# Attention's gathered tables hold two vector components twice, and the sum of a tile's rows is one operation

## The reference

```python
s_n, v_n = _equiv_layernorm(s, v, gamma_s, beta_s, gamma_v)
msg_s = (s_n @ Ws_src)[src] + (s_n @ Ws_dst)[dst]
msg_v = einsum('ncx,cd->ndx', v_n, Wv_src)[src] + einsum('ncx,cd->ndx', v_n, Wv_dst)[dst]
m1_s, m1_v = _cg_tp(msg_s, msg_v, y0, y1, ...)   # products with y, a dot and a cross product of msg_v and y1
a = ...                                          # one logit an edge and head, from m1_s
alpha = softmax of a over the edges with the same dst
h = ...                                          # values an edge, from m1 through a second _cg_tp
agg = segment_sum(alpha * h, dst)
```

## Time and profile before

| what | before |
|---|---|
| median of 3 runs | 25516.59 us |
| lowest and highest | 25451.02 and 25548.4 us |
| span of the profiled execution | 25427.1 us |
| its own time beside the span | the page gives none but the span |
| busy in the span: PE, DVE, ACT, POOL | 19679.3, 19154.8, 12590.5, 12879.8 us |
| node stage ahead of attention | about 6212 to 6580 us of the span |
| edge stage of attention | about 6580 to 17446 us of the span |

### The profile page before, as it was taken

The page is one execution under the profiler, slowest core; times in us unless marked ns, Lnnn a source line. Parts: engine busy times, 40 slices in busy tenths (PEclk is TensorE's granted clock), DMA queues, the critical chain, the costliest instruction groups (busy, mean ns, idle before and its releaser), DMA issues. The chain is left out here.

```text
span 25427.1 us, 480526 instructions
## 1 busy us (share of the span) xinstructions
PE 19679.3 (77%) x108650; PEld 15218.6 (60%) x108650; DVE 19154.8 (75%) x58214; ACT 12590.5 (50%) x42770; POOL 12879.8 (51%) x13907
## 2 busy tenths in 40 slices
PE   1466566565888889899989899985677799677799
PEld 1223222223677777778778777774555588555588
DVE  8333588887777778788878787878777688777688
ACT  0233344443577777777777777773333322333322
POOL 2777655664444444444444444442777500777500
PEclk6677788888999999999999999997999999999999
DMA  0466555555322222222222222223222200222200
GB/s 34 138 172 172 139 111 110 109 109 113 113 73 73 72 74 74 73 74 76 76 73 76 72 76 74 74 74 88 66 61 61 48 6 7 66 61 61 48 6 6
DMA packets 1776894, 1962.61 MB, mean 77 GB/s; under 512 B 754160, under 2 KB 1451744, under 8 KB 1776192
## 3 DMA queue, kind: packets, MB, share of 16 engines
q0 software_dynamic: 567456, 1314.26, 19.5%
q1 hardware_dynamic: 1209376, 647.65, 11.0%
HBM read 1399.54 MB, written 561.06 MB: 77 GB/s over the span
## 5 line engine op out<-in xcount | busy, mean ns | idle before, releaser
L1521 PE MATMUL e_sums<-e_feat,e_same 128*128 128x272 f32 x13824 | 3438.4, 403 | 1357.7 <-ACT e_feat L1542 1231.4
L1503 POOL DMA_INDIRECT e_rows<-x,e_take x3456 | 3609.3, 1044 | 1120.4 <-issue 1047.2
L1521 PEld LDWEIGHTS e_sums<-e_feat,e_same 128*128 128x128 f32 x13824 | 2593.6, 192 | 2202.1 <-issue 1590.7
L581 PE MATMUL e_sums<-e_feat,e_same 128*128 128x480 f32 x3456 | 1962.0, 724 | 1357.2 <-DVE e_feat L649 1357.2
L1049 PE MATMUL e_ps_m<-ident,e_m 128*128 128x128 f32 x12960 | 2092.9, 286 | 1073.6 <-ACT e_m L1122 1062.0
L565 POOL DMA_INDIRECT e_rows<-table,e_take x1728 | 1933.0, 1119 | 1347.0 <-issue 1300.8
L1116 ACT ACTIVATE e_m<-e_th,e_yt 128x64 f32<-128x64 f32 x6480 | 2324.4, 430 | 186.6 <-issue 9.4
L1049 PEld LDWEIGHTS e_ps_m<-ident,e_m 128*128 128x128 f32 x12960 | 1452.8, 145 | 1449.5 <-DVE e_m L1245 772.5
L581 PEld LDWEIGHTS e_sums<-e_feat,e_same 128*128 128x128 f32 x3456 | 803.0, 244 | 2516.8 <-issue 2411.3
L1007 POOL DMA_INDIRECT e_srow<-src_table,e_at x1620 | 1647.3, 1017 | 1248.9 <-POOL e_at L1002 952.5
L600 ACT ACTIVATE e_feat<-e_feat,e_pay 128x64 f32<-128x64 f32 x5184 | 1284.8, 334 | 1806.9 <-DVE e_feat L624 1717.1
(11 more groups left out here) (307 smaller groups left out, 53270.3 us busy)
## 6 DMA issues: line engine op xcount, KB each, us to landing
e_pay<-pay_rows SPq DMA_DIRECT2D x432, 470.0 KB, 3.9
order_keys<-key_row SPq DMA_DIRECT2D x810, 128.0 KB
e_keys<-key_row SPq DMA_DIRECT2D x1620, 64.0 KB, 3.0
e_rows<-x,e_take POOLq DMA_INDIRECT x3456, 2.6
order_feat<-in_attr_T SPq DMA_DIRECT2D x810, 64.0 KB, 3.6
comb<-n_comb SPq DMA_DIRECT2D x300, 164.0 KB, 1.9
e_rows<-table,e_take POOLq DMA_INDIRECT x1728, 4.0
pay_rows<-order_stage,order_put POOLq DMA_INDIRECT x1620
```

The costliest lines, as they stand in the source:

```text
L581: ins = pe.matmul(sums[b][q // G][:, 0:AGG0], same[b][:, q, :], feat[b][:, q, 0:AGG0], start=q % G == 0, stop=q % G == G - 1)
L1503: pool.indirect_dma_start(out=rows[t.j][:, q, :], out_offset=None, in_=x, in_offset=bass.IndirectOffsetOnAxis(ap=take[t.j][:, q:q + 1], ax ...
L1521: ins = pe.matmul(sums[b][q // G][:, 512 * h:512 * h + HALF], same[b][:, q, :], feat[b][:, q, h * HALF:(h + 1) * HALF], start=q % G == 0, ...
```

## The change

The projection part of the tables gets 64 more columns. `MSG` = D + 2 x CV = 224 columns hold the scalars and x y z x y; `COMB` becomes 224 + 168 = 392. The weight matrix `w1_tab` gets the blocks that yield x and y once more (`again`), so that `WT` is 2 x 448 wide instead of 2 x 320. `src_table`, `combs`, `ts`, `comb`, `srow` and `crow` get wider with it, and the four maxima and the sums in a comb row move 64 columns to the right. The two operations that sum a tile's rows become one of 224 columns.

```diff
-COMB = D + SMW
+MSG = D + 2 * CV
+COMB = MSG + SMW
...
-        WA, WX, WT = ph.sb("WA", [P, 4, 192]), ph.sb("WX", [P, 2, 192]), ph.sb("WT", [P, 2, 2 * D])
+        WA, WX, WT = ph.sb("WA", [P, 4, 192]), ph.sb("WX", [P, 2, 192]), ph.sb("WT", [P, 2, 2 * MSG])
...
-                            ins = pe.matmul(ps_c[:, 0:2 * D], nrmT[c.j][:, q * P:(q + 1) * P], WT[:, q, :], start=q == 0, stop=q == 1)
+                            ins = pe.matmul(ps_c[:, 0:2 * MSG], nrmT[c.j][:, q * P:(q + 1) * P], WT[:, q, :], start=q == 0, stop=q == 1)
...
-                        act.activation(ts[c.j][:, :], ps_c[:, 0:D], ACT.Copy)
-                        act.activation(comb[c.j][:, 0:D], ps_c[:, D:2 * D], ACT.Copy).then_inc(out_set, 1)
+                        act.activation(ts[c.j][:, :], ps_c[:, 0:MSG], ACT.Copy)
+                        act.activation(comb[c.j][:, 0:MSG], ps_c[:, MSG:2 * MSG], ACT.Copy).then_inc(out_set, 1)
...
-        srow = [ph.sb(f"srow{k}", [P, D]) for k in range(SLOTS)]
+        srow = [ph.sb(f"srow{k}", [P, MSG]) for k in range(SLOTS)]
...
-                        dve.tensor_tensor(mv[ka][:, 0:D], srow[a.j][:, :], crow[a.j][:, 0:D], ALU.add)
-                        dve.tensor_tensor(mv[ka][:, D:D + 2 * CV], srow[a.j][:, CS:CS + 2 * CV], crow[a.j][:, CS:CS + 2 * CV], ALU.add).then_inc(mv_set, 1)
+                        dve.tensor_tensor(mv[ka][:, :], srow[a.j][:, :], crow[a.j][:, 0:MSG], ALU.add).then_inc(mv_set, 1)
...
-                            sp.dma_start(runs[b.j][:, k, :], combs[k][where, D:COMB]).then_inc(runs_in[b.j], 16)
+                            sp.dma_start(runs[b.j][:, k, :], combs[k][where, MSG:COMB]).then_inc(runs_in[b.j], 16)
...
-        table0, src_table = dram("table0", [NP, D]), dram("src_table", [NP, D])
+        table0, src_table = dram("table0", [NP, D]), dram("src_table", [NP, MSG])
...
-    a["w1_tab"] = _blocks(256, 2 * D, [(0, 0, g["Ws_src"]), (0, D, g["Ws_dst"])]
-                          + _per_component(64, 64, g["Wv_src"]) + _per_component(64, D + 64, g["Wv_dst"]))
+    again = [(64 + CV * k, at + D + CV * k, w) for at, w in ((0, g["Wv_src"]), (MSG, g["Wv_dst"])) for k in range(2)]
+    a["w1_tab"] = _blocks(256, 2 * MSG, [(0, 0, g["Ws_src"]), (0, MSG, g["Ws_dst"])]
+                          + _per_component(64, 64, g["Wv_src"]) + _per_component(64, MSG + 64, g["Wv_dst"]) + again)
```

More of the change, by code:

```diff
@@ L732, in nodes_after_0 @@
         stats = [ph.sb(f"stats{k}", [P, 24]) for k in two]
-        ts = [ph.sb(f"ts{k}", [P, D]) for k in two]
+        ts = [ph.sb(f"ts{k}", [P, MSG]) for k in two]
         comb = [ph.sb(f"comb{k}", [P, COMB]) for k in two]
@@ L877, in _ @@
                     dve.memset(agg[k][:, AGG0:4 * P], 0.0)
-                    dve.memset(comb[k][:, D:D + 4], LOW)
-                    ins = dve.memset(comb[k][:, D + 4:COMB], 0.0)
+                    dve.memset(comb[k][:, MSG:MSG + 4], LOW)
+                    ins = dve.memset(comb[k][:, MSG + 4:COMB], 0.0)
                 ins.then_inc(blank, 1)
@@ L940, in edge_layer1 @@
         yt = [ph.sb(f"yt{k}", [P, 10]) for k in range(SLOTS)]
-        srow = [ph.sb(f"srow{k}", [P, D]) for k in range(SLOTS)]
+        srow = [ph.sb(f"srow{k}", [P, MSG]) for k in range(SLOTS)]
         crow = [ph.sb(f"crow{k}", [P, COMB + 4]) for k in range(SLOTS)]
-        mv, qs, qv = pair("mv", [P, CS + 5 * CV]), pair("qs", [P, 2 * CS]), pair("qv", [P, 3 * CV])
+        mv, qs, qv = pair("mv", [P, MSG]), pair("qs", [P, 2 * CS]), pair("qv", [P, 3 * CV])
         by_y1, by_y2, pairs = pair("by_y1", [P, 9 * CV]), pair("by_y2", [P, 9 * CV]), pair("pairs", [P, 4 * CV])
@@ L1159, in step @@
                         act.activation(hw[k][:, :].rearrange("p (h m) -> p h m", h=4)[:, :, 0:1], dif[k][:, 4:8].unsqueeze(2), ACT.Exp).then_inc(den_set, 1)
-                        act.activation(crow[c.j][:, D:D + 4], mx[k][:, 4:8], ACT.Copy).then_inc(kept, 1)
+                        act.activation(crow[c.j][:, MSG:MSG + 4], mx[k][:, 4:8], ACT.Copy).then_inc(kept, 1)
                     if a.exists():
@@ L1269, in step @@
                             dve.wait_ge(kept, c.count(-1))
-                        dve.tensor_tensor(mx[kc][:, 4:8], row[:, D:D + 4], mx[kc][:, 0:4], ALU.max).then_inc(mn_set, 1)
+                        dve.tensor_tensor(mx[kc][:, 4:8], row[:, MSG:MSG + 4], mx[kc][:, 0:4], ALU.max).then_inc(mn_set, 1)
                     if c.exists():
@@ L1274, in step @@
                             dve.wait_ge(ex_set, c.count(-1))
-                        old = row[:, D:D + 4]
+                        old = row[:, MSG:MSG + 4]
                         dve.tensor_tensor(dif[kc][:, :].rearrange("p (g h) -> p g h", g=2),
-                                          bass.AP(old.tensor, old.offset, [old.ap[0], [COMB - D, 2], [1, 4]]),
+                                          bass.AP(old.tensor, old.offset, [old.ap[0], [COMB - MSG, 2], [1, 4]]),
                                           bcast(mx[kc][:, 4:8].unsqueeze(1), (P, 2, 4)), ALU.subtract).then_inc(dif_set, 1)
@@ L1280, in step @@
                         dve.wait_ge(ex_set, c.count(1))
-                        acc = row[:, D + 4:COMB].rearrange("p (h m) -> p h m", h=4)
+                        acc = row[:, MSG + 4:COMB].rearrange("p (h m) -> p h m", h=4)
                         dve.tensor_tensor(acc, acc, bcast(ex[kc][:, 0:4].unsqueeze(2), (P, 4, HD)), ALU.mult).then_inc(scaled, 1)
@@ L1297, in step @@
                         dve.wait_ge(scaled, c.count(1))
-                        dve.tensor_tensor(row[:, D + 4:COMB], row[:, D + 4:COMB], ps_g[:, 0:4 * HD], ALU.add).then_inc(row_set, 1)
+                        dve.tensor_tensor(row[:, MSG + 4:COMB], row[:, MSG + 4:COMB], ps_g[:, 0:4 * HD], ALU.add).then_inc(row_set, 1)
                 run_steps(dve, step, 4, SLOTS, NT, COUNTS)
```

## The result

| | median | lowest to highest | runs |
|---|---|---|---|
| before | 25483.81 us | 25420.36 to 25548.4 | 4 |
| the change | 26455.18 us | 26430.02 to 26490.26 | 4 |

The ratio is 1.0389, with a 95% interval of 1.0367 to 1.0410. The change makes the kernel 971 us slower; 172 us slower was forecast.

The account below looks back on a forecast made before the run. The prediction took POOL's ring through the scatter's landing as the bound. It added 162 us at the edges and 10 us at the nodes, 172 us on 25516.6, for 25689 us, range 25530 to 25860.

Parts of the forecast that it names:

- What bounds the kernel: In the edge stage, POOL's ring of waits, closed by the scatter's landing, sets the pace: 6.72 us a tile.
- What is taken away: DVE's two sums at the edges become one of 391 ns: 0.07 to 0.15 us a tile, worth 0 on the path.
- What is added at the edges: Wider rows make the scatter land 0.10 us later a tile (bounds 0.06 and 0.19): 162 us in all.
- Rival 2: At the edges, the table gather delays the scatter, both growths adding: 0.19 us or more a tile, 25850 us; chance 0.10.
- Rival 3: In the edge stage, DVE sets the pace and tiles get 0.07 to 0.15 us shorter: 25404 to 25269 us; chance 0.08.
- Phase between DVE and POOL: Where POOL's operations fall against DVE's in the edge stage: gives or takes 40 us at most, left out of the sum.
- The nodes: In `nodes_after_0`, the wider table matmul and evictions add 10 us, bounds 0 and 30.

Follow-up runs that it names:

- e8: The kernel before with POOL's index copy split, so the source gather no longer waits for the scatter's landing; 24727.16 us, ratio 0.9732.
- e2: The kernel before, rows and transfers still narrow, with one DVE sum of 224 columns (second operand 32 gathered columns repeated); 25824.67 us, ratio 1.0136.
- e1: The changed kernel with its one sum split again into two (160 and 64 columns), tables and transfers still wide; 26239.55 us, ratio 1.0303.
- e4: The kernel before with one more wait, so SP's loads go out at POOL's index copy, ahead of the scatter; 25028.03 us, ratio 0.9826.
- e3: The changed kernel with one more wait, so SP's loads go out at POOL's index copy, ahead of the scatter; 25439.69 us, ratio 0.9991.
- e7b: The changed kernel with its sum split again into two and SP's loads issued at POOL's index copy; 25286.95 us, ratio 0.9944.

## Why the prediction was wrong

**What bounds the kernel** was right: POOL's ring through the scatter's landing sets the pace, its groups fill the stage before and after, and e8 shows it by taking the landing out. So was the direction.

**What is taken away** was right in size (392 ns, DVE's busy time down) and wrong in worth. "On the path it is worth 0" is a step that failed: it rested on POOL not waiting for DVE. POOL does not, but SP does: DVE's mask operation releases SP's loads, and their moment decides how long the scatter takes. The table gather's landing starts DVE's step when DVE waits for it, and then the load trails the gather's issue by some 8.8 us (12020.96 - 12012.14 in the changed kernel; 12015.84 - 12007.06 in the one before). When DVE is behind, it comes later: the median over all tiles is 8.83 us in the changed kernel and 9.04 in the one before. The next scatter is issued 1.25 us and one period behind that gather. A period of 6.3 us leaves 1.25 us between scatter and load, one of 7.4 us only 0.15. So a late landing makes the period that brings the next scatter and load together, which is the chain of 86% against 5% that the table's traces show. In a tenth of the tiles the load comes less than 8.66 us behind the gather in the kernel before, 8.59 in e2, 8.77 in e1 and 8.69 in the changed kernel: the shorter sum takes 0.07 to 0.08 us off. e2 measured what I had put at nothing: 357 us.

**What is added at the edges** is the step that weighed most, at "I take **0.10**" with its bounds of 0.06 and 0.19: the idle time before the index copy grew by 978 / 1620 = 0.60 us a tile. As a price by the byte the 0.10 was near: 2.55 to 2.69 us for undisturbed scatters, 0.13 between e4 and e3, 259 / 1620 = 0.16 with the copy in e7b. But the landing of the kernel before was not one value. I read its median of 2.5 us and used the maximum of 4.3 only as a spread. The mean of the wait before the copy, 2.07 us, stands 0.25 to 0.3 over the 1.78 and 1.82 of the tile shown; that gap was 27% of the tiles at 1 us each, the most telling number in the rows, and I passed over it. What the wider rows do beside their own 0.14 us is to widen the window in which a load makes the scatter late: at 0.75 to 1.0 us between scatter and load, 32 of 164 narrow scatters landed late, and 150 of 167 wide ones. They make the ring 0.14 us longer, but they also put SP's load 0.11 us later behind the gather (8.66 to 8.77 us), so by distance the two nearly cancel. Why the window is wider is open; the one packet more for each engine fits it, and no run separates that. The copy held up by DVE's product is a third term that the sum had put at nothing; it costs nothing in the changed kernel, and up to 246 us where no load meets the scatter.

**Rival 2** had the form right (the scatter's data held up by another transfer) and the partner and the price wrong: I looked only at the table gather on the same queue. **Rival 3** is turned round: a shorter DVE step made the kernel slower (e2). **Phase between DVE and POOL** was put at some 40 us; in e3 it is 246 us, since the copy there meets DVE's product. In the changed kernel itself it is nothing, 355.5 against 354.2 us. **The nodes** cost 4 us, where 10 were taken. Had the two kinds of landing been seen, the direction would have stood and the size would still have been open: no row of the kernel before tells how far the stage would tip.

## What to carry to other kernels

Where a DMA's landing is in a ring, compare the mean of the wait for it with its usual length: a gap can mean that it has two lengths, and then ask which other queue's transfer stands beside the long ones. Transfers that are needed only much later should be issued at a moment tied to the ring, away from what it waits for, and not whenever their buffer comes free; here one wait gained 1.7%, and taking the landing off the path by splitting the wait that put it there gained 2.7%. A change off the critical path can still cost, if it moves the moment at which other engines' transfers go out.

## What the runs showed of the hardware

A load of 64 KB in rows of 512 bytes on SP's queue delays a scatter of 128 rows on GpSimd's queue by about 1 us (2.55 to 3.54 us narrow, 2.69 to 3.64 wide). Both are busy for less than that: SP's three loads of a tile together fill 6.2% of 10866 us, 0.42 us an engine and tile, and the scatter some 0.5 by the prediction's estimate. The scatter's landing depends on their distance like a step: of narrow ones all of 48 were late at 0.5 to 0.75 us, and none of 279 at 1.0 to 1.25. Whether the chip's queues take turns, or the keys' writes stand ahead of the scatter's last packets, these runs do not tell.

POOL's copy of 3 columns took 0.49 us instead of 0.19 when DVE's product with two SBUF inputs had started 0.01 us before it, and ended 0.05 us behind it. In e4, 596 copies began with over 0.1 us left of a DVE product that reads one of its inputs from PSUM (L1234), and took 0.19 us in the mean. That is the lock on the shared port pair that the Trainium skill describes (SBUF — State Buffer, SBUF: two separate sides: whichever of the two starts first gets it for the whole instruction, a DVE operation with two SBUF inputs only against a GpSimd one that reads SBUF). The traces agree with it for POOL's copy. For DVE they do not show it: in e4, 581 of DVE's products of 288 columns began 25 ns or more behind the start of a copy, while it was running, and took 452 ns in the mean, as all others did.
